# Front block's sums on TensorE, and linear attention's normalisation by tiles beside its first products

## The reference

```python
# layer 0: layer norm over the 256 channels, plus a scaled position table, then a Mamba block
pos = jnp.concatenate([jnp.sin(sinu), jnp.cos(sinu)], axis=-1) * pos_scale
h = _layernorm(seq, ln_g, ln_b) + pos
xz = h @ in_proj_w.T
...
# layer 1: x = x + linear_attention(_gn(x)), group norm with 32 groups
qkv = (t @ Wqkv + bqkv)                  # t: normalised tokens
q = relu(q) * scale;  k = relu(k)
ctx = einsum('bhnd,bhne->bhde', k, v);  out = einsum('bhnd,bhde->bhne', q, ctx)
img = depthwise_conv_3x3(out) + dw_b
t = _repbn(t + img @ Wproj + bproj, bn1...)     # (x - m) * rsqrt(v + eps) * g + b + alpha * x
ff = gelu(t @ Wfc1 + bfc1) @ Wfc2 + bfc2
t = _repbn(t + ff, bn2...)
```

## Time and profile before

| | |
|---|---|
| time, median of 3 runs | 5443.99 us (5424.35 to 5455.64) |
| the profiled execution's own time | 5449.95 us |
| its span, from the first instruction to the last | 5448.2 us |
| busy share: PE, DVE, ACT, POOL | 85%, 64%, 40%, 43% |
| mean granted TensorE clock | 0.95 |

### The profile page before, as it was taken

One profiled execution on the slowest core, in us unless ns is written; L12 is line 12 of the kernel. 1 busy time (PEld: TensorE's weight loads), 2 busy tenths in 40 slices (PEclk: granted clock), 3 DMA queues, 4 the chain that ended last, 5 costly groups with the idle time before them and its releaser, 6 DMA issues. The chain is left out here.

```text
span 5448.2 us, 50177 instructions
## 1 busy us (share of the span) xinstructions
PE 4625.2 (85%) x14182; PEld 2509.8 (46%) x14183; DVE 3462.0 (64%) x5154; ACT 2158.7 (40%) x3550; POOL 2321.9 (43%) x2118
## 2 busy tenths in 40 slices
PE   5877888988778888699899899488699899996797
PEld 2333333433333333355455555355355455554576
DVE  4999999999999999769389365254332200103233
ACT  4655666666656666232232322111122212213232
POOL 5888888888889888401102200452000000003111
PEclk8999999999999999999999999689799999998898
DMA  4344444433444443200100000100112000001222
GB/s 141 114 122 151 125 129 130 139 113 115 138 139 131 131 134 112 69 31 0 57 31 15 31 4 21 44 13 18 45 44 73 34 0 2 0 0 45 65 72 96
DMA packets 222888, 391.83 MB, mean 72 GB/s; under 512 B 36146, under 2 KB 205912, under 8 KB 218300
## 3 DMA queue, kind: packets, MB, share of 16 engines
q1 hardware_dynamic: 214524, 383.83, 21.9%
q0 software_dynamic: 8128, 5.27, 0.6%
HBM read 337.13 MB, written 58.23 MB: 73 GB/s over the span
## 5 line engine op out<-in xcount | busy, mean ns | idle before, releaser
L916 POOL TENSOR_TENSOR DBU<-DU,BB 128x461 f32<-128x461 f32 (+1 forms) x1280 | 1371.8, 1086 | 297.9 <-DVE PS L960 284.7
L606 PE MATMUL PS<-G,ident 128*128 128x461 f32 (+1 forms) x2560 | 1146.9, 574 | 374.9 <-DVE G L971 372.3
L960 DVE TENSOR_TENSOR_SCAN PS<-PS,HC,DBU 128x461 f32<-128x461 f32 (+1 forms) x1024 | 1148.9, 1166 | 7.4 <-ACT PS L778 6.0
L778 ACT ACTIVATE PS<-DT,alog 128x461 f32<-128x461 f32 (+1 forms) x1280 | 825.2, 645 | 722.8 <-DVE PS L960 722.0
L606 PEld LDWEIGHTS PS<-G,ident 128*128 128x128 f32 x2560 | 456.3, 191 | 1030.1 <-DVE G L971 803.7
L971 DVE TENSOR_TENSOR G<-PS,CB 128x461 f32<-128x461 f32 (+1 forms) x1280 | 785.4, 623 | 5.0 <-PE PS L606 5.0
L3033 DVE TENSOR_TENSOR X<-X,PS 128x768 f32 x12 | 11.4, 954 | 556.1 <-PE PS L3000 556.1
L2989 PE MATMUL PS<-QT,N 128*128 x864 | 313.1, 490 | 4.7 <-ACTq L3006 4.7
L1349 POOL TENSOR_TENSOR X<-X,FF x12 | 41.7, 3475 | 636.8 <-ACT EV L1344 636.8
L3000 PE MATMUL PS<-AT,XT 128*128 128x384 f32 x864 | 310.3, 486 | 0.0
L3064 POOL TENSOR_TENSOR xs<-X 128x384 f32 x12 | 11.8, 992 | 696.8 <-issue 398.9
(11 more groups left out here) (431 smaller groups left out, 7271.5 us busy)
## 6 DMA issues: line engine op xcount, KB each, us to landing
BB<-proj_dram SPq DMA_DIRECT2D x256, 461.0 KB, 3.9
CB<-proj_dram SPq DMA_DIRECT2D x64, 922.0 KB, 6.1
BB<-proj_dram SPq DMA_DIRECT2D x64, 460.0 KB, 4.8
ew<-in_l_w SPq DMA_DIRECT2D x16, 1024.0 KB, 6.6
CB<-proj_dram SPq DMA_DIRECT2D x16, 920.0 KB, 6.2
w_fc<-in_l_w_fc SPq DMA_DIRECT2D x4, 2048.0 KB, 11.8
XI<-xi_dram SPq DMA_DIRECT2D x8, 928.0 KB, 5.0
xi_dram<-XI SPq DMA_DIRECT2D x8, 922.0 KB, 6.6
```

The source lines that it names most:

```text
L606: pe.matmul(PS[:, j, :wide(g)], k.ident[:], G[:, S % 4, :wide(g)], start=False, stop=(n == DS - 1))\
L778: act.activation(DA(S), DT[:, j, :wide(g)], ACT.Exp, scale=w.alog[:, chunk(g)[1], j, n:n + 1]).then_inc(da_done, 1)
L916: pool.tensor_tensor(DBU[:, S % 4, :wide(g)], DU[:, j, :wide(g)], BB[:, 2 * u + n % 2, :wide(g)], ALU.mult).then_inc(dbu_done, 1)
L960: dve.tensor_tensor_scan(flow(HS(S), g), flow(DA(S), g), flow(DBU[:, S % 4, :wide(g)], g), start, ALU.mult, ALU.add).then_inc(h_done, 1)
```

## The change

In the front block POOL's two additions a tile go; PE instead multiplies both halves by `mean_w` and sums them in PSUM, for the mean and for the squares. The buffer `xs` and two semaphores go. The position table is scaled tile by tile, two operations of 384 columns at each of the steps 2 to 7.

In linear attention the normalisation, the scales SB and the filter matrices `dwd` move from the first block into the second. DVE normalises tiles 0 and 1 (two operations of 384 columns each), then tile t + 2 ahead of each of the first four bias additions; PE waits for tile t // 3 ahead of slice t. SB comes after the eighteenth bias addition, `dwd` is POOL's list of the second block. In the first block ACT takes the square root of the variance ahead of the four others. The bias of the scales moves behind ACT's copies of IMG. Three semaphores are added.

```diff
@@ front block
-                        pool.tensor_tensor(xs[:, s % DEEP, :], tile(s)[:, 0, :], tile(s)[:, 1, :], ALU.add)\
-                            .then_inc(x_summed, 1)
...
-                        pool.tensor_tensor(sq[:, v % DEEP, 0, :], sq[:, v % DEEP, 0, :], sq[:, v % DEEP, 1, :], ALU.add)\
-                            .then_inc(sq_summed, 1)
...
-                        if v == 0:
-                            pool.wait_ge(pos_done, KC)
+                        pool.wait_ge(pos_done, KC * min(v + 1, NT))
...
-                        pe.matmul(k.PS[:, s % DEEP, :T], k.mean_w[:], xs[:, s % DEEP, :], start=True, stop=True)\
-                          .then_inc(mean_ready, 1)
+                        for c in range(KC):
+                            mm = pe.matmul(k.PS[:, s % DEEP, :T], k.mean_w[:], tile(s)[:, c, :], start=(c == 0),
+                                           stop=(c == KC - 1))
+                        mm.then_inc(mean_ready, 1)
...
+                        for c in range(KC):
+                            mm = pe.matmul(k.PS[:, DEEP + v % DEEP, :T], k.mean_w[:], sq[:, v % DEEP, c, :], start=(c == 0),
+                                           stop=(c == KC - 1))
+                        mm.then_inc(var_ready, 1)
...
-                    if s == 3:
-                        act.wait_ge(pos_in, 48)
+                    if 2 <= s < 2 + NT:
+                        if s == 2:
+                            act.wait_ge(pos_in, 48)
                         for c in range(KC):
-                            act.activation(pos[:, c, :], pos[:, c, :], ACT.Identity, bias=gb[:, c, 1:2], scale=pscale[:])\
-                               .then_inc(pos_done, 1)
+                            at = pos[:, c, (s - 2) * T:(s - 1) * T]
+                            act.activation(at, at, ACT.Identity, bias=gb[:, c, 1:2], scale=pscale[:]).then_inc(pos_done, 1)
@@ linear attention, first block
-                    dve.reciprocal(sq[:], sq[:])
-                    dve.drain()
-                    for i in range(KC):
-                        dve.tensor_scalar(k.N[:, i, :], k.X[:, i, bass.ds(b * L, L)], g[:, i, 0:1], g[:, i, 3:4],
-                                          ALU.subtract, ALU.mult)
...
-                    pool.wait_ge(l1_loaded, 112)
-                    for t in range(TAPS * TAPS):
-                        pool.tensor_scalar(dwd[:, t, :], k.ident[:], dw[:, 1, t:t + 1], None, ALU.mult)
@@ linear attention, second block
+                            if t % (T // P) == 0:
+                                pe.wait_ge(n_ready, t // (T // P) + 1)
...
+                    pe.wait_ge(dwd_done, 1)
                     for c in range(HALF):
...
+                    act.wait_ge(sb_done, 1)
...
+                    def norm(c):
+                        for i in range(KC):
+                            op = dve.tensor_scalar(k.N[:, i, c * T:(c + 1) * T], k.X[:, i, bass.ds(b * L + c * T, T)],
+                                                   g[:, i, 0:1], g[:, i, 3:4], ALU.subtract, ALU.mult)
+                        op.then_inc(n_ready, 1)
+
+                    norm(0)
+                    norm(1)
                     for t in range(LT):
+                        if t < NT - 2:
+                            norm(t + 2)
                         dve.wait_ge(kv_ready, t + 1)
```

More of the change, by code:

```diff
@@ L1159, in _ @@
                     dve.reciprocal(g[:, :, 3], g[:, :, 3])
-                    dve.reciprocal(sq[:], sq[:])
-                    dve.drain()
-                    for i in range(KC):
-                        dve.tensor_scalar(k.N[:, i, :], k.X[:, i, bass.ds(b * L, L)], g[:, i, 0:1], g[:, i, 3:4],
-                                          ALU.subtract, ALU.mult)
[L1165 to L1170, removed]
-                        dve.tensor_tensor(SB[:, :, w, 1], vec[:, :, bn + 1], SB[:, :, w, 1], ALU.subtract)
-                        dve.tensor_scalar(SB[:, :, w, 0], SB[:, :, w, 0], alpha[:, w:w + 1], None, ALU.add)
                 @block.tensor
@@ L1181, in _ @@
                 def _(act):
+                    act.wait_ge(vg_done, 1)
+                    act.activation(g[:, :, 3], g[:, :, 2], ACT.Sqrt, bias=k.eps5[:]).then_inc(root_done, 1)
                     act.wait_ge(l1_loaded, 112)
@@ L1185, in _ @@
                         act.activation(sq[:, :, 2 + w], vec[:, :, BN + 4 * w + 3], ACT.Sqrt, bias=k.eps5[:])
-                    act.wait_ge(vg_done, 1)
-                    act.activation(g[:, :, 3], g[:, :, 2], ACT.Sqrt, bias=k.eps5[:]).then_inc(root_done, 1)
                 @block.gpsimd
@@ L1191, in _ @@
                     pool.memset(IMG[:], 0.0)
[L1192 to L1194 removed]
             fresh(nc, used)
[L1198 removed]
+            used = sems(nc, own, "n_ready", "sb_done", "dwd_done", "q_ready", "q_done", "kv_ready", "kv_added", "kv_done", "kv_used", "ctx_ready",
                         "ctx_done", "img_ready", "img_done", "cv_ready", "cv_done", "part_done", "pr_ready", "tt_raw",
                         "bias_done", "tt_done")
[L1201 removed]
+            (n_ready, sb_done, dwd_done, q_ready, q_done, kv_ready, kv_added, kv_done, kv_used, ctx_ready,
              ctx_done, img_ready, img_done, cv_ready, cv_done, part_done, pr_ready, tt_raw,
@@ L1205, in linear_attention_block, with _ @@
             with nc.Block() as block:
+                @block.gpsimd
+                def _(pool):
+                    for t in range(TAPS * TAPS):
+                        op = pool.tensor_scalar(dwd[:, t, :], k.ident[:], dw[:, 1, t:t + 1], None, ALU.mult)
+                    op.then_inc(dwd_done, 1)
                 @block.tensor
@@ L1267, in _ @@
                 def _(act):
-                    for o in range(KC):
-                        act.activation(SB[:, o, 1, 1:2], vec[:, o, BFC2:BFC2 + 1], ACT.Identity, bias=SB[:, o, 1, 1:2],
-                                       scale=SB[:, o, 1, 0:1]).then_inc(bias_done, 1)
                     for t in range(LT):
@@ L1286, in _ @@
                                .then_inc(img_done, 1)
+                    act.wait_ge(sb_done, 1)
+                    for o in range(KC):
+                        act.activation(SB[:, o, 1, 1:2], vec[:, o, BFC2:BFC2 + 1], ACT.Identity, bias=SB[:, o, 1, 1:2],
+                                       scale=SB[:, o, 1, 0:1]).then_inc(bias_done, 1)
                     for c in range(HALF):
@@ L1312, in _ @@
                         dve.tensor_tensor(KV[:, t % RING, :], k.PS[:, 2 + t % 2, :], bkv[:], ALU.add).then_inc(kv_added, 1)
+                    dve.reciprocal(sq[:], sq[:])
+                    dve.drain()
+                    for w in range(2):
+                        bn = BN + 4 * w
+                        dve.tensor_tensor(SB[:, :, w, 0], vec[:, :, bn], sq[:, :, w], ALU.mult)
+                        dve.drain()
+                        dve.tensor_tensor(SB[:, :, w, 1], vec[:, :, bn + 2], SB[:, :, w, 0], ALU.mult)
+                        dve.drain()
+                        dve.tensor_tensor(SB[:, :, w, 1], vec[:, :, bn + 1], SB[:, :, w, 1], ALU.subtract)
+                        dve.tensor_scalar(SB[:, :, w, 0], SB[:, :, w, 0], alpha[:, w:w + 1], None, ALU.add)
+                    dve.drain().then_inc(sb_done, 1)
                     dve.wait_ge(ctx_ready, 1)
```

25 lines of the change are left out of this document (6 added, 19 removed).

## The result

The changed kernel takes 5408.89 us (median of 4 runs, 5406.18 to 5415.45), the kernel before 5445.76 (4 runs, 5424.35 to 5455.64): ratio 0.9941, 95% interval 0.9919 to 0.9962. That is 36.9 us less (20.7 to 44.1 by that interval). The forecast was 5416.6 with a range of 5400 to 5436, and 27.4 us of gain. The profiled execution has a span of 5404.4 us instead of 5448.2.

What follows compares the result with a forecast made beforehand. In the front, POOL's additions, the DVE operations they stretch and the whole-table scaling bound; in linear attention's first block, POOL's `dwd`. Gains 15.3 + 12.3 - 0.2 = 27.4 us take 5443.99 to 5416.6, range 5400 to 5436.

Steps and rivals of the forecast that it cites:

- The sum: Whole kernel: 15.3 us from the front plus 12.3 from linear attention, less 0.2 for semaphores, 27.4 us gained.
- The 0.8 us added for PE's first products: Front block: PE's first products would run at half clock, so the block's end was put 0.8 us later, at 49.9.
- Tile 0 was priced at 0.65 us: Linear attention's second block: PE waits for two DVE operations of 0.30 us each and a hand-over of 0.05.
- What was said to be hidden: Linear attention's second block: filters, tiles 2 to 5 and scales lie beside other work; scales cost 0, 1.1 us spare.
- Contention at the block's head: Linear attention's second block: `dwd` and the first normalisation start together; POOL would pay, so DVE was charged nothing.
- the other reading: Linear attention's second block: DVE lets a 0.6 us POOL operation pass ahead of each of its two; 2.4 us less gain.
- The first (L214 on top of L284): Front block: POOL's L214 slows DVE's L284, so the front ends 6 to 8 us later; 5424 us, chance 0.15.
- The second (PE at half clock bounds the front): Front block: 48 products at 1.29 us end it at about 73.5, 8.3 us lost; 5440 in all, chance 0.06.
- The third (second block late): Linear attention: POOL's 7.6 us covered other preparation, such as next instructions; up to half of 12 us lost, 5423, chance 0.09.
- The fourth: Linear attention: PE stutters waiting for tiles and stays at half clock through 18 slices; 78 us slower, 5495, chance 0.03.
- The fifth (nothing moves): Whole kernel: what the blocks gain is waited away at the engines' meetings between them; 5444 us, chance 0.03.

Runs made afterwards that it cites:

- only the filters moved: From the kernel before, only the filter matrices `dwd` move into linear attention's second block; 5400.12 us against 5411.05, ratio 0.9974.
- the scales first: The changed kernel with the scales SB computed in linear attention's first block again, behind ACT's fourth root; 5369.49 us, ratio 0.9923 to the kernel before.
- the filters later: The changed kernel with POOL's filter matrices started only behind the sixth normalised tile; 5396.08 us, ratio 0.9933 to the kernel before.
- the clock kept up: The changed kernel with 31 unread products of 128 columns on PE in each linear-attention batch; 5395.77 us, ratio 0.9937 to the kernel before.
- the run of the products alone: From the kernel before, only POOL's front additions become second PE products, the position table still scaled whole; 5419.98 us against 5426.02, ratio 0.9977.

## Why the prediction was right, point by point

**The front block: right, with an offset inside.** The sum had 15.3 us; the first Mamba product came 15.5 earlier. L276 ran at its free pace, 1.13 to 1.15 us a pair, in eight of twelve rounds; the other four took 1.35 to 1.86. The pieces of the table, priced by L1297 at 1.20 start to start, took 1.19 (24.92 to 26.11). ACT's round took 3.00 instead of 3.1. The square of tile 8 started at 35.11 where 35.3 had been worked out, the last square at 42.45 (42.6), the last Exp ended at 46.12 (46.0), and ACT's constants at 49.10 (49.1). The 0.8 us added for PE's first products was not needed: the first eight records of the mean took 5.49 us, but the third square started at 15.92, against 15.97 before, and the granted clock is 1.00 from 14 to 44 us. In its place stood a term that the sum had at nothing. DVE was to be done at 48.3, with the last scaling and position additions undisturbed; beside POOL's additions they took 1.86 and 1.81 us, and DVE ended at 49.75. (The 1.81 for the last two L292 could be read in the earlier trace rows.) From there to the next product it took 1.70 us instead of 1.81, with two semaphores fewer. So the right total came in part by luck: an allowance that wasn't needed filled a stretch that was left out.

**Linear attention: right in mechanism, its size too large.** 12.3 us were forecast, 10.5 measured (765.6 to 755.1), and 10.4 by the run of this part alone. The borders came out nearly as forecast: 6.04 us shorter in the first batch and 5.90 in the second, where 6.15 each had been worked out. Inside the first, two errors all but cancel. Tile 0 was priced at 0.65 us from L1163's length; it took 1.00, since 384 columns cost 0.47 and not 0.30: the fixed part is larger than I took. Against that, ACT's fourth root ended 13.34 us behind the last output and not 13.63, as in the kernel before. What was missing in the sum is that half clock at the first products, which both kernels have, need not last as long in both. It lasted longer in the changed kernel: the second bias addition came 5.7 to 6.7 us behind the first product in all six batches of its three profiles, and 5.2 to 5.5 in all ten batches of the five profiles with the old code (the run with this part alone had 5.4 and 6.3, with only the filters moved 6.7 and 5.8, with the scales first 5.5 and 5.4, with the filters later 5.2 and 6.4). The slices took 1.5 and 0.7 us more, of which 0.6 came back behind them: 11.94 - 2.18 + 0.64 = 10.4. With the clock kept up the second bias addition came at 3.7 in all four batches, so the clock is what bounds there.

**What was said to be hidden was hidden.** The filters: PE waited for them nowhere. The scales: the context was done at 2310.51, PE used it at 2311.89, 1.4 us later, where 1.1 had been worked out; moved back, they cost 3.3 to 3.9 us. Contention at the block's head: DVE paid 0.09 us for an operation at most, not 0.6; the 2.4 us of the other reading did not come. POOL's filter operations took up to 0.85 us beside the tiles, and 0.60 to 0.62 where they started behind them. GPSIMD Engine Reference, in the Trainium skill (section 1, the row on SBUF interfaces), names such contention, for DVE instructions in a 2-port mode or with two SBUF inputs. The front agrees for two SBUF inputs (L284, 2.71 us a pair beside POOL and 1.14 alone); in which mode the tile operations ran, no run shows.

**The sum and the measurement.** 27.4 us were forecast. The two touched stretches gained 15.5 + 10.5 = 26.0 in the profiles, and the two halves measured alone 15.6 + 10.4 = 26.0. The whole was measured three times: 36.9, 22.9 and 38.2 us (5411.05 to 5372.85). So the size is right for the touched stretches. The 10 us by which the first and third measurement exceed the forecast must lie elsewhere, and the untouched stretches vary: the edge sums between 300 and 364 us, the Mamba block between 2191 and 2200, with the same code. For the first measurement the two profiles show it (11.3 us in the edge sums, 7.4 behind them). For the third they don't: its interval (29.2 to 46.0 us) lies above 26.0, the run with only the filters moved exceeded its touched stretch beside the same kernel before, and no profile of the kernel before was taken there. Whether the changed programs gain something in untouched stretches in that session stays open; on the same chip earlier, the two halves and the whole did not. Of the 0.59% of the first measurement the forecast can claim the 0.48% that 26.0 us are.

**The rivals.** The first (L214 on top of L284) is seen in four of twelve rounds, such as a pair of 1.53 us at 37.05 and the last one of 1.86 at 46.16. Up to tile 8 ACT set the pace, not DVE, but the longer last pair has a part in DVE's late end. The second (PE at half clock bounds the front) did not occur: the granted clock was 1.00 from 14 to 44 us, with PE busy 92% of it. Its mechanism, half clock, occurred elsewhere: at the first products of the Mamba block and of linear attention. The third (second block late) did not occur: it was 0.92 us instead of 0.85 from ACT's root to the first tile operation. The fourth needed 0.73 us for a tile operation; 0.47 was measured, further on the way than the 0.30 that I assumed, and PE did not stutter: from the second bias addition on a slice took 2.16 us, as before. The fifth (nothing moves) is refuted by both touched stretches.

**Open.** It is not known why the Mamba block takes 2191 us in some executions and 2200 in others. The starts of one of its lines, compared between profiles, keep their distance for long stretches and part in two, from about 700 to 1140 us and from 1710 to 2150. In the second the granted clock differs, as two executions of the changed kernel show for the same piece of the program, first the shorter block:

```profile
1988.90:2032.80 43.90, 37.00 (x90) 16.23 (x90) 43.90 (x67) 30.17 (x47) 41.15 (x39) 1.00 0.56 180
```

```profile
1994.60:2040.40 45.80, 39.15 (x88) 17.02 (x89) 45.49 (x70) 30.01 (x47) 42.69 (x40) 0.93 0.57 180
```

43.9 us at full clock, 45.8 with a part at half. What makes the clock fall in one execution and not in the other was not tried. Nor was it tried why the edge sums differ between executions and chips, or why full clock comes later behind the changed border.

## What to carry to other kernels

A wait that seems to be one engine's is often held by several that end close to each other: moving the filters alone gave 3.4 us, all three pieces 10.5. List what is last, next to last, and after that before pricing a move. Take an engine's small additions away and look also at the neighbour that they stretch: in the run of the products alone DVE's scaling fell from 2.7 to 1.14 us a pair though nobody had edited it. Price a cut into small pieces by a row of the small size; a long operation divided by its columns leaves out the fixed part. And where a kernel's whole time scatters by more than the effect, compare the length of the touched stretch in the profiles: here it repeats within 1 us while the total moves by 60. Look also at what follows a shortened wait: behind the shorter border the clock rose later, and that took part of the gain.

## What the runs showed of the hardware that was not expected

A `tensor_scalar` of DVE on 384 f32 columns takes 0.47 us, on 2304 columns 1.47, so about 0.27 us of it do not depend on the columns. Unread products that keep PE at 2.4 GHz paid for themselves at this border between blocks: 31 of them a batch, put where PE waited, saved 3.0 us a batch. And such a gain need not last: 2.8 us won at the start of the Mamba block were kept for 600 us and then lost in two stretches in which the granted clock was 0.83 and 0.61 instead of 1.00. The same slices behind the same border also found full clock at different times in the two batches of one execution: in the changed kernel's first profile the second bias addition came 6.7 and 5.9 us behind the first product.
